# Bit-weighted sums of both weight chunks on TensorE, with the weights laid out bit by bit at launch

## What is computed

```
x = x + attention(layernorm(x), ctx, ctx)
x = x + layernorm(x) @ weight.T + bias

soft   = sigmoid(pweight) - sigmoid(nweight)            # (1024 out, 1024 in, 4 bits)
weight = einsum('oin,n->oi', soft, exps * sigmoid(mask_weight)) * scale
```

## Time and profile before

| | |
|---|---|
| median of 3 runs | 1241.85 us (1240.62 to 1242.14) |
| the profiled execution | 1242.96 us |
| its span, first to last instruction | 1241.1 us |
| busy: PE / PEld | 1114.6 / 814.5 us |
| busy: DVE / ACT / POOL | 1027.6 / 925.9 / 716.2 us |
| mean granted clock of TensorE | 0.977 |
| bytes moved | 190.88 MB, 47.14 MB of them in the first 200 us |

### The profile page before, as it was taken

How to read it: one execution, slowest core, us unless ns; L and a number is a source line. 1 busy time by engine, 2 the same in 40 slices (tenths; PEclk the granted TensorE clock), 3 DMA queues, 4 the chain that set the end, 5 groups by cost and what they waited for, 6 DMA issues and landing times. The chain is left out here.

```text
span 1241.1 us, 28269 instructions
## 1 busy us (share of the span) xinstructions
PE 1114.6 (90%) x10820; PEld 814.5 (66%) x10820; DVE 1027.6 (83%) x1480; ACT 925.9 (75%) x1930; POOL 716.2 (58%) x774
## 2 busy tenths in 40 slices
PE   3587679789999999989999999999999999999988
PEld 3576565556666677666766777776776676676663
DVE  5889987888888887888887887888888887888862
ACT  5787766768878778877787787777787787787750
POOL 4576544636544987644545887654546986462351
PEclk9888789999999999999999999999999999999999
DMA  8699752756666897656657978665668886665442
GB/s 306 204 299 279 262 137 60 160 116 148 128 126 126 206 167 180 134 115 144 143 100 172 199 146 173 146 136 103 145 130 172 176 182 134 147 118 89 90 86 68
DMA packets 387189, 190.88 MB, mean 154 GB/s; under 512 B 358640, under 2 KB 358640, under 8 KB 387056
## 3 DMA queue, kind: packets, MB, share of 16 engines
q1 hardware_dynamic: 386048, 189.05, 67.0%
q10 hardware_dynamic: 1008, 0.04, 0.0%
HBM read 67.15 MB, written 16.78 MB: 68 GB/s over the span
## 5 line engine op out<-in xcount | busy, mean ns | idle before, releaser
L534 ACT ACTIVATE p<-slot,mx 128x512 f32<-128x512 f32 (+7 forms) x512 | 377.7, 746 | 165.4 <-DVE mx L650 109.3
L650 DVE TENSOR_REDUCE mx<-slot 128x1 f32<-128x640 f32 (+7 forms) x352 | 356.5, 1015 | 30.8 <-PE slot L419 29.2
L466 PE MATMUL ffnb<-wt,yt 128*128 128x512 f16 x1464 | 373.5, 382 | 2.9 <-DVE ring L712 1.5
L656 DVE SCALAR_TENSOR_TENSOR pt<-ptb,pt 128x512 f16<-128x512 f32 (+1 forms) x504 | 281.4, 598 | 100.8 <-ACT pt L550 100.7
L415 PE MATMUL slot<-kt,qt 128*128 128x128 f16 (+3 forms) x1056 | 270.7, 286 | 19.1 <-ACT p L534 11.8
L416 PE MATMUL slot<-kt,qs 128*128 128x128 f16 (+3 forms) x1056 | 269.8, 285 | 0.0
L550 ACT ACTIVATE pt<-ptb 128x512 f16<-128x512 f32 (+1 forms) x504 | 239.2, 527 | 30.6 <-PE ptb L429 29.0
L891 POOL TENSOR_TENSOR att<-osb 128x256 f32<-128x256 f32 x128 | 97.1, 758 | 271.7 <-ACT osb L557 265.2
L429 PE MATMUL ptb<-id,p 128*128 128x128 f32 x1700 | 240.1, 280 | 12.8 <-DVE pt L656 11.6
L466 PEld LDWEIGHTS ffnb<-wt,yt 128*128 128x128 f16 x1464 | 137.1, 98 | 103.7 <-issue 4.1
L448 PE MATMUL oacc<-v,pt 128*128 128x128 f16 x1700 | 180.2, 221 | 25.5 <-ACT osb L557 11.9
(11 more groups left out here) (105 smaller groups left out, 1551.8 us busy)
## 6 DMA issues: line engine op xcount, KB each, us to landing
ring<-in_x_dram SPq DMA_DIRECT2D x32, 512.0 KB, 4.1
cin<-in_ctx_dram SPq DMA_DIRECT2D x32, 512.0 KB, 4.6
out_dram<-ring SPq DMA_DIRECT2D x32, 512.0 KB, 3.4
qs<-qt SPq DMA_DIRECT2D x124, 128.0 KB, 2.8
v<-in_L_ffn_pweight_dram SPq DMA_DIRECT2D x22, 512.0 KB, 6.3
kt<-in_L_ffn_nweight_dram SPq DMA_DIRECT2D x16, 512.0 KB, 7.8
v<-in_L_ffn_nweight_dram SPq DMA_DIRECT2D x6, 512.0 KB, 5.9
kt<-in_L_ffn_pweight_dram SPq DMA_DIRECT2D x5, 512.0 KB, 4.0
```

The lines of the kernel that those rows point to most:

```text
L466: last = pe.matmul(dst, yt[:, k % 2, a * KT_N + kk, :], wt[:, c, kk, half * 512:half * 512 + 512], start=r == 0, stop=r == 3 * KT_N - 1)
L534: last = nc.scalar.activation(p32[:, j.par, hh * j.keys:(hh + 1) * j.keys], slot[:, j.par, base:base + j.keys], ACT.Exp, bias=mx[:, j.par, ...
L650: nc.vector.tensor_reduce(mx[:, j.par, 0:j.heads], src[:, 0:j.heads, 0:j.keys], AX_X, ALU.max, negate=True).then_inc(mx_ready, 1)
L656: nc.vector.scalar_tensor_tensor(pt[:, j.par, j.blocks + blocks.start:j.blocks + blocks.stop, :], ptb[:, c % 2, 0:P * len(blocks)].rearran ...
```

## The change

The launch hands the kernel both weight tensors as one, `weights_in`, of shape (32 chunks, 128, 2, 4, 256): per chunk 128 **input** features on the partitions, and for each partition 8 KB in one run, first pweight then nweight, each by bit, and for each bit 256 output rows side by side. So the weights arrive transposed, and the columns of one bit are contiguous. The work of this layout is done by the launch and is not in the device time; no arithmetic is in it.

- `load_w`: one DMA of 1 MB per chunk in place of two of 512 KB. It waits for the chunk that was in the place (`w_summed`), not for the unit.
- `chunk_tanh`: one tanh over 2048 columns in place of two over 1024.
- Differences: the even chunk's is always VectorE's (`first_difference`), the odd chunk's always GpSimd's, 16 and 16.
- `weights_sum` is gone, with its four operations, and the transposes L484.
- TensorE sums both chunks: per chunk and bit one matmul, with the diagonal of the coefficient stationary and 256 contiguous columns of the difference moving, 2 x 4 matmuls per unit, each written to half of `ffnb`.
- The places move: each is 8 KB in one run; `coef_diag` is in `ring` now, `p16` and `ptd` share the buffer `pd`. Waits of tile work that reuses a place are for `w_lo`, `w_summed` in place of `w_turned`.

```diff
             def load_w(w):
-                reached(sp, w_turned, (w - PAIRS) // 2 + 1)
-                sp.dma_start(pairs[w % PAIRS][0], pw_t[w // NWCH, w % NWCH]).then_inc(w_in[w % PAIRS], 16)
-                sp.dma_start(pairs[w % PAIRS][1], nw_t[w // NWCH, w % NWCH]).then_inc(w_in[w % PAIRS], 16)
+                reached(sp, w_summed, w - PAIRS + 1)
+                sp.dma_start(pairs[w % PAIRS], weights_in[w]).then_inc(w_in[w % PAIRS], 16)
...
                 elif t >= 5:
-                    sp.wait_ge(w_turned, UNITS)
+                    sp.wait_ge(w_lo, UNITS)
                 sp.dma_start_transpose(kt16[:, t % K_PLACES], v16[:, t % V_PLACES]).then_inc(k_in[t % 2], 16)
...
                 reached(pe, w_lo, u)
-                pe.wait_ge(w_sum, u + 1)
-                for b in range(2):
-                    pe.transpose(ffnb[:, b * P:(b + 1) * P], pairs[2 * u % PAIRS][1][:, b * P:(b + 1) * P], id32[:, :])
-                pe.wait_ge(d_ready, differences_to(2 * u + 1))
-                a = pairs[(2 * u + 1) % PAIRS][0].rearrange("p (k n) -> p k n", n=NBITS)
-                for b in range(2):
+                for w in (2 * u, 2 * u + 1):
+                    if w % 2:
+                        pe.wait_ge(d_ready, u + 1)
+                    else:
+                        pe.wait_ge(w_sub, u + 1)
+                    diff = pairs[w % PAIRS][:, 0]
+                    c0 = WCH * (w % 2)
                     for n in range(NBITS):
-                        last = pe.matmul(ffnb[:, (b + 2) * P:(b + 3) * P], a[:, b * P:(b + 1) * P, n],
-                                         coef_diag[:, n, :], start=n == 0, stop=n == NBITS - 1)
-                last.then_inc(w_turned, 1)
+                        last = pe.matmul(ffnb[:, c0:c0 + WCH], coef_diag[:, n, :], diff[:, n, :],
+                                         start=n == 0, stop=n == NBITS - 1)
+                    last.then_inc(w_summed, 1)
...
             def chunk_tanh(w):
-                act.wait_ge(w_in[w % PAIRS], 32 * (w // PAIRS + 1))
-                for half in pairs[w % PAIRS]:
-                    last = nc.scalar.activation(half, half, ACT.Tanh, scale=0.5)
-                last.then_inc(th_ready, 1)
+                act.wait_ge(w_in[w % PAIRS], 16 * (w // PAIRS + 1))
+                place = pairs[w % PAIRS]
+                nc.scalar.activation(place, place, ACT.Tanh, scale=0.5).then_inc(th_ready, 1)
...
+            def first_difference(u):
+                dve.wait_ge(th_ready, 2 * u + 1)
+                place = pairs[2 * u % PAIRS]
+                nc.vector.tensor_tensor(place[:, 0], place[:, 0], place[:, 1], ALU.subtract).then_inc(w_sub, 1)
...
                 if j.n + 1 < UNITS:
-                    weights_sum(j.n + 1)
+                    first_difference(j.n + 1)
...
-                if j.n + 1 < UNITS and on_pool(2 * j.n + 2):
-                    difference(2 * j.n + 2)
                 if j.n > 1 and JOBS[j.n - 2].closes_group:
                     add_attention(JOBS[j.n - 2].group)
```

More of the change, by code:

```diff
@@ L36 @@
 WCH = 256
-NWCH = DM // WCH
 CHUNKS = 32
@@ L151, in y_at @@
             if s == (Y_LATE[k][part] if k in Y_LATE else (Y_HI, Y_LO)[part - 1][steps(t)])]
[L154 to L161, removed]
 def turn_k_step(t):
@@ L229, in build, with chunk_place @@
         bvec = sb("bvec", [P, 8], F32)
[L232 to L238, removed]
+        p16 = pd[:, 0]
+        ptd = pd[:, 1].rearrange("p (k c) -> p k c", c=P)
+        def chunk_place(places):
+            return places.bitcast(F32).rearrange("p (a n k) -> p a n k", a=2, n=NBITS)
+        pairs = [chunk_place(v16[:, 8:10].rearrange("p a h c -> p (a h c)")),
+                 chunk_place(kt16[:, 7:9].rearrange("p a h c -> p (a h c)")),
+                 chunk_place(kt16[:, 5:7].rearrange("p a h c -> p (a h c)")),
+                 chunk_place(v16[:, 6:8].rearrange("p a h c -> p (a h c)")),
+                 chunk_place(pd[:, :, :].rearrange("p a c -> p (a c)")),
+                 chunk_place(yt[:, :, :, :].rearrange("p a k c -> p (a k c)"))]
+        coef_diag = ring[:, 6, 0:NBITS * P].rearrange("p (n q) -> p n q", n=NBITS)
         swapped = v16[:, 2]
@@ L242, in build, with weight_cols @@
         bits = y16[:, 1, 0, :].bitcast(F32).rearrange("p (a n) -> p a n", a=2)
-        bdiag = as_f32(kt16, 4).rearrange("p (j q) -> p j q", j=8)
+        bdiag = kt16[:, 4].rearrange("p h c -> p (h c)").bitcast(F32).rearrange("p (j q) -> p j q", j=8)
         coef = small[:, 14:18]
+        def weight_cols(part, u):
+            half, k = divmod(u, KT_N)
+            return wt[:, part, k, 2 * WCH * half:2 * WCH * (half + 1)]
         slot = stack.enter_context(nc.psum_tensor("slot", [P, 2, 1024], F32))
@@ L273, in build @@
         bias_added, ffn_done, res_done = sem("bias_added"), sem("ffn_done"), sem("res_done")
-        th_ready, d_ready, w_sub, w_mul, w_sum, w_turned, w_hi, w_lo = (
-            sem("w_" + n) for n in ("tanh", "diff", "sub", "mul", "sum", "turned", "hi", "lo"))
+        th_ready, d_ready, w_sub, w_summed, w_hi, w_lo = (
+            sem("w_" + n) for n in ("tanh", "diff", "sub", "summed", "hi", "lo"))
         pool_const, coef_tanh, coef_step, bias_step = (
@@ L571, in c_split @@
                     act.wait_ge(pv_done, batch_end(t - V_PLACES))
-                elif t >= 5:
-                    act.wait_ge(w_turned, UNITS)
+                elif t >= 6:
+                    act.wait_ge(w_lo, UNITS)
                 nc.scalar.copy(v16[:, t % V_PLACES, :, 0:D], cin[:, :].rearrange("p (h d) -> p h d", d=D)
@@ L791, in _ @@
             maxima(JOBS[1])
-            weights_sum(0)
+            first_difference(0)
             for j in JOBS:
@@ L922, in _ @@
             q_prepare(1, 0)
-            difference(0)
             difference(1)
@@ L969, with give @@
     arrays, args = {}, []
-    for name in _INS:
-        a = _np.ascontiguousarray(inputs[name])
+    def give(name, a):
+        a = _np.ascontiguousarray(a)
         arrays[f"in_{name}_dram"] = a
         args.append(nc.dram_tensor(f"in_{name}_dram", a.shape, mybir.dt.from_np(a.dtype), kind="ExternalInput").ap())
+    give('x', inputs['x'])
+    give('ctx_2048', inputs['ctx_2048'])
+    both = _np.stack([inputs['L0_ffn_pweight'], inputs['L0_ffn_nweight']])
+    both = both.reshape(2, 2, 2, WCH, KT_N, P, NBITS).transpose(1, 4, 2, 5, 0, 6, 3)
+    give('weights', both.reshape(CHUNKS, P, 2, NBITS, WCH))
+    for name in _INS:
+        give(name, inputs[name])
     args.append(nc.dram_tensor("out_0_dram", (B, SEQ, DM), F32, kind="ExternalOutput").ap())
```

50 lines of the change are left out of this document (12 added, 38 removed).

## The result

The changed kernel takes 1213.6 us, median of 4 runs (1213.2 to 1213.8), against 1242.0 us (1240.6 to 1242.3, 4 runs) on the same chip: a ratio of 0.9771, 95% interval 0.9758 to 0.9783, or -28.4 us. The forecast was 1225 with a range of 1210 to 1238. So the time lies in the range, but the gain is 28 us where 17 were forecast. The profiled execution took 1213.7 us, 1211.9 of them span.

The account below looks back on a forecast made before the run. VectorE was taken to bound 30 to 166 us (121 of 136); relieved, DMA's 113 plus 8 idle make 121, -15, and -2 in the last jobs: 1243 - 17 = 1226, forecast 1225 by the median, range 1210 to 1238.

Parts of the forecast that it names:

- rival (a): Weight-making stretch: loads get cheaper (DMA 89 us) and ScalarE's 103.5 plus 8 idle bounds, 112 us; total 1216; chance 0.15.
- The bound: From 30 to 166 us VectorE is the full engine, 121.2 of 136 us; from 200 us on it is TensorE.
- The sum: Stretch to the last weights' landing: VectorE 65 to 75, PE 85 to 99, ScalarE 103.5, DMA 113 plus 8 idle: 121.
- the forecast 160 to 164: Sign to look for: ScalarE's last copy of a unit at some 160 to 164 us, against 179.6 before.
- L714 behaved: VectorE's new difference was to take 1.25 us, few over 3; at worst each is held by GpSimd some 2.4 us.
- the later part: From 200 us on, TensorE work starting when the weights are done: nothing there gives the gain back.
- The bound from below: TensorE's new sums (L488): if the weight load alone set the pace, 2.1 us a unit; the estimate was 3.6.
- The DMA term: Weight-making stretch: DMA keeps 113 us busy, larger loads saving nothing, and 8 of 23 us idle time stays: 121 us.
- 16 differences, 20.4 us at the same price: VectorE's differences after the change, against 10.2 us for eight before; with 69.5 us of operations gone, net -59 us.
- (c): Rival: slower, as TensorE falls to the lower clock throughout, 10.2 us a job against 9.4: 1254; chance 0.07.
- (d): Rival: single buffer ffnb (matmuls, copy, split, next matmuls) keeps jobs from shortening: no change, 1242; chance 0.05.
- (b): Rival: small gain, 19 of 23 us idle DMA time kept by SyncE's queue order, or differences holding each other: 1236; chance 0.10.

Follow-up runs that it names:

- one_product: The kernel before with the even chunk's bit sum cut to its first product, three of VectorE's four operations left out: ratio 0.9863, -17 us.
- narrow_sums: The changed kernel with TensorE's sums in 16 float32 matmuls of 128 columns per unit in place of 8 of 256: ratio 0.9764.
- split_loads: The changed kernel with each chunk loaded by two DMAs of 512 KB in place of one of 1 MB: ratio 0.9786.
- old_io: The changed kernel with two 512 KB loads and two tanh of 1024 columns per chunk, as before the change: ratio 0.9796.
- loads_first: The changed kernel with the weights' loads ahead of the tile loads of the same step in SyncE's queue; ran twice: ratios 0.9751 and 0.9746.
- half_loads: The changed kernel with only the first half (pweight) of chunks 6 to 31 loaded: ratio 0.9738.
- old_all: The changed kernel with old loads and tanh, differences shared as before, and TensorE's sums in matmuls of 128 columns: ratio 0.9816.
- old_shares: The changed kernel with differences shared as before the change, 24 on GpSimd and eight on VectorE: ratio 0.9785, runs from 1210 to 1221 us.
- own_difference: The kernel before with three of the four bit operations left out and every even chunk's difference made by VectorE: ratio 0.9824.

## Why the prediction was right, and where it was not

**The number.** The time lies in the stated range, but not where the prediction put its weight: it gave 0.60 to 1217 to 1235, and 1213.6 lies in the part of the range that it kept for rival (a) with 0.15, 11 us from the forecast and 2 from that rival's 1216. (a)'s cheaper loads turn out to be the smaller part of the difference. That the range held is in part luck.

**The bound.** It was VectorE between 30 and 166 us. Two experiments from opposite sides put 17 us on its sum, the whole of what was forecast. The sum fits one_product, which is VectorE's relief alone: its last copy stands at 162.5, in the forecast 160 to 164, and from 30 to 149 us, about when its last weights land, the DMA engines are busy 0.94 x 119 = 112 us and idle 7, where the sum had 113 and 8. The change does more than that. Its waits changed as described, L714 behaved (1.4 us, few held), the later part gave nothing back, and the last copy moved to 152.4. Of the 29 us by which the span is shorter, 23.7 lie between first and last copy, where 17 were forecast, 3.5 before and 2 behind, where nothing was.

**TensorE.** A pass of 256 float32 columns was to last as 512 float16 ones: 0.215 us apart at the upper level and 0.43 at the lower. The profile has both, in TensorE's timeline of the kernel after:

```profile
83.81 1.89 PE L488 MATMUL ffnb<-kt,ring 128*128 128x256 f32 x8
...
118.15 3.78 PE L488 MATMUL ffnb<-pd,ring 128*128 128x256 f32 x8 [3.54 <-DVE wt L718]
```

Eight passes take 1.89 us, less 0.38 for the first, over 7: 0.216. The others ran at a granted clock of 0.50, behind a wait of 3.5 us: 3.78, less 0.80 for the first, over 7, is 0.43. In all 68.9 us for 16 units, where the sum at the old clock mix said 57.6 + 17 = 75, and at the new clock of 0.89 says 57.6 + 12 = 69. The bound from below (2.1 us a unit) was far off. Whether TensorE's price matters at all no run tests, since narrow_sums left it as it was; at 86 of 108 us busy, and with 19 us of waits for the split, it has room.

**ScalarE.** The tanh of a chunk takes 1.94 us, and the two before took 1.99: half of the 0.1 us that the sum allowed for. It is busy 96 of 108 us, 89%, where the sum had 86%.

**The DMA term was mis-sized, both parts of it.** The sum let 113 us of DMA time and 8 idle stand, 121. Measured: 0.97 x 108 = 105 busy and 3 idle, 108. The idle time: I kept a third of the 23 us, most of which lay ahead of the context loads. SyncE's waits there (the row of L294 above, against L295 in the earlier trace rows) now run mostly while earlier loads are still in flight: the share is 1.00 from 80 to 85 us, before the context load at 86.1, and it is under a half only at 50 to 54 us (0.34 and 0.40), 72 to 74 (0.39) and 130 to 132 us (0.23). The busy time: I saw no price that larger loads would save, since 402 GB/s were had with the small ones. The rate when busy went from 262 / 0.83 = 316 to 317 / 0.97 = 327 GB/s, and goes back to 310 to 319 in split_loads and old_io. That is 3 to 4%, or some 4 us; the other 4 are bytes, as the stretch from 30 to 138 us holds 34.2 MB where the one from 30 to 166 held 35.6. Of these 1.4 MB only 0.4 had moved before 30 us; 1.0 moves after 138. The cheaper bytes go the way of rival (a), whose DMA term fell by 24 us, and are a sixth of it. The Trainium skill's fit of 2 us and bytes over 436 GB/s (DMA: Bandwidth & Descriptors, Anatomy of one DMA — SWDGE (gpsimd) path) is made for single transfers from GpSimd's queue; here, with several in flight, 32 fewer transfers saved 4 us and not 64.

**The start was left out of the sum.** The prediction put it at nothing, saying of GpSimd's new order only that it can bring the attention sums forward. The first copy came 3.5 us earlier. In the new order no difference of GpSimd runs beside VectorE's second split of a context tile. Timelines of before (two rows) and after (one):

```profile
21.46 2.47 POOL L906 TENSOR_TENSOR v<-v 128x1024 f32<-128x1024 f32 x1 [0.40 <-ACT v L596]
...
22.34 2.66 DVE L698 TENSOR_TENSOR v<-cin,v 128x1024 f16<-128x1024 f32 x1 [0.63 <-ACT v L574]
...
20.44 1.23 DVE L695 TENSOR_TENSOR v<-cin,v 128x1024 f16<-128x1024 f32 x1 [1.19 <-ACT v L573]
```

The split took 2.66 us and takes 1.23. A part is scatter: in the six profiles of kernels with the change's start (both of loads_first, half_loads, split_loads, old_io, narrow_sums) the first copy stands between 33.4 and 34.9, and in those with the old order of differences at 36.0 (one_product), 36.3 (before and old_all) and 37.2 (old_shares). own_difference, the kernel before but for the order and the bit sums left out, has 33.3 and a split of 1.37 us; in one_product the difference fell beside another operation of VectorE, and the split took 1.21. So some 2 us belong to the order and up to 2 to chance.

**The wait for GpSimd was missed.** The step "16 differences, 20.4 us at the same price" counted work. It also removes waits: before the change they cost 9.5 us of idle time in VectorE's row in total, and in one_product they had grown to 19.6. What that is worth stays open, since own_difference, without them, is only 1.6 us faster between the copies.

**Rivals.** (c) is refuted: the clock of the stretch rose from 0.84 to 0.89. (d): the ring through `ffnb` does not stop the gain, but it is what stands now, as TensorE's waits run through VectorE's split to ScalarE's copy, and the one kernel in which the copy was moved is the fastest (by 3 us over loads_first, which is not clear of noise). (b) is refuted: of the idle DMA time 3 us stand, where it had 19. (a): in time the change is even past it. In mechanism the truth lies between the forecast and (a), by ScalarE's and the DMA's terms, 96 and 105 us in 108, where (a) had 103.5 in 112 and 89.

## What to carry to other kernels

When the fullest engine of a stretch is relieved, the new time is the largest of the other sums plus what idle time its queue really has: take idle time that comes from waiting for the relieved engine out with it, don't keep a share of it (23 us here became 3). Look at the start too: what a new order takes out of the way of the first unit is gained once, whatever the bound of the stretch is. A wait that disappears is not a gain by itself: the 19.6 us for GpSimd went, and 10 us of work and 10 of waits for ScalarE's tanh came in their place. And when several parts are each worth about what a measurement can tell apart (+3, +2 and -1 us here), undo them together before calling them free: together they were +6, clear of noise.

## What the runs showed of the hardware that was not expected

A float32 pass of 256 contiguous moving columns with a diagonal as the stationary operand costs about as much as a pass of 128 columns whose stationary block has a stride of four numbers: 71.6 against 71.1 us for all units. But they behave differently. L489's passes before were 3.8 to 4.0 us a unit at either clock level; L488's follow the clock, 0.216 us a pass at 2.4 GHz and 0.43 at 1.2. With 128 columns and the same diagonal, a pass is 0.11 us at 2.4 GHz (16 in 1.95 us, narrow_sums), half of L489's 0.24. That the stride of the stationary block makes up this difference is a reading of these rows; no run changed the stride alone.

With loads of 1 MB and 8 KB runs, the DMA engines move 321 to 332 GB/s of their busy time from 30 to 138 us, and with loads of 512 KB 303 to 319, although several loads are in flight in both; where the loads are densest, at 10 to 20 us, it is 411 to 416 against 392 to 405.
